# Wide edge one-hot compares on VectorE alone, and an fp32 gather of node rows, in a two-layer graph network kernel

## What is computed

```python
def layer0(x, src, dst, weight, bias):          # x is layernorm + relu of the input
    adj = zeros(256, 256); adj[src, dst] = 1; adj[dst, src] = 1; adj += eye
    dinv = 1 / sqrt(adj.sum(1))
    return (dinv[:, None] * adj * dinv[None, :]) @ (x @ weight) + bias

def layer1(x, idx_i=src, idx_j=dst, f=edge_attr_20, rcut=edge_weight, Yr=edge_attr_4):
    hs, hv = x[:, :128] @ w_in2f_s, einsum(x[:, 128:], w_in2f_v)     # 32 + 3*32 node channels
    s, v = hs[idx_j], hv[idx_j]                                     # gather: one row per edge
    W = (ssp(f @ W1 + b1) @ W2 + b2) * rcut                         # edge filters, 6 kinds x 32
    edge = [s*ys*W0, (v.yv)*W1, s*yv*W2, v*ys*W3, ...]
    agg = segment_sum(edge, idx_i, 256)                             # scatter: sum over edges
    return two dense layers of agg

x = x + layer0(relu(layernorm(x)), ...)
x = x + layer1(relu(layernorm(x)), ...)
```

## Time and profile before

| what | value |
|---|---|
| median of 3 runs (lowest, highest) | 89.17 us (88.24, 89.19) |
| profiled execution: span from its first to its last instruction | 86.5 us |
| median less that span | 2.7 us |
| busy: DVE, PE, POOL, PE weight loads, ACT | 73.4, 70.9, 55.1, 54.2, 40.6 us |
| share of the chain that ended last: DVE, PE, POOL, DMA | 57%, 17%, 5%, 6% |

### The profile page before, as it was taken

How to read it: one execution, slowest core, us unless ns; L and a number is a source line. 1 busy time by engine, 2 the same in 40 slices (tenths; PEclk the granted TensorE clock), 3 DMA queues, 4 the chain that set the end, 5 groups by cost and what they waited for, 6 DMA issues and landing times.

```text
span 86.5 us, 1513 instructions
## 1 busy us (share of the span) xinstructions
PE 70.9 (82%) x545; PEld 54.2 (63%) x545; DVE 73.4 (85%) x180; ACT 40.6 (47%) x60; POOL 55.1 (64%) x58
## 2 busy tenths in 40 slices
PE   4928999999359979999189999998778697999930
PEld 1204367388123536899089999996667595989620
DVE  1039999999997769998999999999999999992490
ACT  0140216929997025593702535271643639970520
POOL 2019999998940299989992789183664748970000
PEclk9999999999999999999965999999999999999996
DMA  2899999800000000000000000000000000000024
GB/s 8 249 319 368 373 438 426 312 0 0 0 0 8 0 0 0 0 0 0 0 0 8 0 0 0 0 8 0 0 8 0 0 0 0 8 4 0 0 91 152
DMA packets 3340, 6.01 MB, mean 69 GB/s; under 512 B 444, under 2 KB 2224, under 8 KB 3204
## 3 DMA queue, kind: packets, MB, share of 16 engines
q1 hardware_dynamic: 2274, 4.93, 16.2%
q10 hardware_dynamic: 1058, 0.98, 3.7%
HBM read 5.39 MB, written 0.52 MB: 68 GB/s over the span
## 4 chain that ended last, share of the span: by engine, by line
DVE 57%; PE 17%; issue 9%; DMA 6%; POOL 5%; ACT 2%; DVEq 0%; POOLq 0%
DVE onehot_dst L372 11%; DVE WY L174 8%; PE bank L682 7%; DMA idx_sb<-idx 6%; DVE WY L172 5%; DVE Os L371 4%; DVE WY L173 3%; DVE dst_bc L501 3%; DVE dst_bc L497 3%; PE bank L622 3%; POOL scales L335 2%; DVE dst_bc L494 2%; DVE dst_bc L495 2%; PE bank L640 2%; DVE Hp L466 2%
## 5 line engine op out<-in xcount | busy, mean ns | idle before, releaser
L682 PE MATMUL bank<-OsR,Mh 128*128 128x256 f32 x68 | 17.7, 297 | 3.3 <-POOL Ml L360 1.6
L682 PE MATMUL bank<-OsR,Ml 128*128 128x256 f32 x68 | 16.7, 281 | 0.0
L360 POOL TENSOR_TENSOR Ml<-dst_bc,Mh 128x512 fp32r<-128x512 f32 x8 | 10.3, 1283 | 9.4 <-ACT Mh L284 9.4
L682 PEld LDWEIGHTS bank<-OsR,Mh 128*128 128x128 f32 x68 | 12.8, 188 | 4.8 <-POOL Ml L364 2.4
L666 PE MATMUL bank<-Hp,onehot_dst 128*128 128x128 bf16 x204 | 14.0, 229 | 2.1 <-issue 2.1
L666 PEld LDWEIGHTS bank<-Hp,onehot_dst 128*128 128x128 bf16 x204 | 12.4, 103 | 2.7 <-issue 2.3
L548 PE MATMUL bank<-onehot_dst,Os 128*128 128x256 bf16 x68 | 10.0, 294 | 4.4 <-DVE onehot_dst L372 4.4
L372 DVE TENSOR_SCALAR onehot_dst<-iota_r,idf 128x256 bf16<-128x256 bf16 x27 | 13.0, 483 | 0.0
L682 PEld LDWEIGHTS bank<-OsR,Ml 128*128 128x128 f32 x68 | 12.8, 189 | 0.0
L548 PEld LDWEIGHTS bank<-onehot_dst,Os 128*128 128x128 bf16 x68 | 6.1, 102 | 8.9 <-DVE onehot_dst L372 7.7
L364 POOL TENSOR_TENSOR Ml<-dst_bc,Mh 128x512 fp32r<-128x512 f32 x7 | 10.4, 1492 | 1.3 <-ACT Mh L286 1.3
(11 more groups left out here) (116 smaller groups left out, 148.4 us busy)
## 6 DMA issues: line engine op xcount, KB each, us to landing
dst_bc<-dst_row SPq DMA_DIRECT2D x1, 2176.0 KB, 12.7
w_sb<-w SPq DMA_DIRECT2D x1, 1024.0 KB, 8.9
x_sb<-x SPq DMA_DIRECT2D x1, 512.0 KB, 5.6
...
idx_sb<-idx SPq DMA_DIRECT2D x1, 162.0 KB, 4.9
...
```

Of the source, the lines that this page charges most:

```text
L360: nc.gpsimd.tensor_tensor(Ml[:, o, 1, 0:n, :], M[:, o, 1, 0:n, :], Mh[:, o, 1, 0:n, :].bitcast(fp32), ALU.subtract).then_inc(q["MlB"], 1)
L682: last = nc.tensor.matmul(bank[4 + b][:, 0:N], part[:, g % RG, b, j, :], OsR[:, g % RG, j, :], start=(t == 0 and part is Mh), stop=(t == T ...
```

## The change

- All edge one-hots are made on DVE, by `tensor_tensor` instead of `tensor_scalar`: one instruction per matrix and wave, over 2, 4, 6, 8, 8, 4 and 2 tiles (`WAVES`). The numbers of the edges are bf16 in pairs (`idp`), so that both inputs end in a dimension of two neighbours. The node row comes ready from memory. One semaphore step per wave.
- The indices are first on SP's queue and smaller; the node row and `w1` go first on ACT's queue; `w1` no longer stands before `x`.
- GpSimd has no one-hots and no `hY`; it makes one extra power on a scratch tile at the start. DVE makes `hY`, after `hW_lo`.
- `OdT` is fp32, compared straight from the int32 row, with no bf16 copy. Its four calls stand after `hY`, and three in a row after `h2T`. The loop's first group has none behind it.
- `H` is scaled by ACT from PSUM to fp32 in SBUF, when `s2` is there; the gather is 2 fp32 matmuls per tile.
- ACT copies filter group 0 after the squares of `h2` instead of before; PE computes it after layer 0's product instead of before.
- `WY` is a ring of 6 groups.

```diff
     RW = 4
+    RY = 6
...
-    PT = T - 7
+    WAVES = ((0, 2), (2, 6), (6, 12), (12, 20), (20, 28), (28, 32), (32, T))
...
-        idx_sb = sb("idx_sb", [P, 2 * T + N], i32)
+        idx_sb = sb("idx_sb", [P, 2 * T], i32)
...
-        idf = sb("idf", [P, 2 * T])
+        idp = sb("idp", [P, 2 * T, 2], bf16)
...
-        dst_b = sb("dst_b", [P, E], bf16)
-        onehot_dst = sb("onehot_dst", [P, T * N], bf16)
-        Od = onehot_dst[:, :].rearrange("p (t n) -> p t n", t=T)
-        OdT = onehot_dst[:, :].rearrange("p (a e) -> p a e", a=NH)
+        OdT = sb("OdT", [P, NH, E])
+        Od = OdT[:, 0, :].bitcast(bf16).rearrange("p (t n) -> p t n", t=T)
...
-        Hr = sb("Hr", [P, NH, C])
-        Hp = [sb(f"Hp{i}", [P, NH, C], bf16) for i in range(3)]
+        H = sb("H", [P, NH, C])
...
-        WY = sb("WY", [P, T, S * F])
+        WY = sb("WY", [P, RY, TG, S * F])
...
         @block.sync
             sp.dma_start(idx_sb[:], idx).then_inc(d_idx, 16)
-            sp.dma_start(w1_sb[:], w1).then_inc(d_w1, 16)
             sp.dma_start(x_sb[:, :, :], x.rearrange("(a p) d -> p a d", p=P)).then_inc(d_x, 16)
...
         @block.scalar
+            act.dma_start(iota_r[:], iota).then_inc(d_iota, 16)
+            act.dma_start(w1_sb[:], w1).then_inc(d_w1, 16)
             act.dma_start(f_sb[:], f_t).then_inc(d_f, 16)
...
-            act.wait_ge(d_dst, 16)
-            nc.scalar.activation(dst_b[:], dst_bc[:], ACT.Copy).then_inc(q["dstb"], 1)
...
                 nc.scalar.activation(hW_hi[:, a, :], bank[a][:, :], ACT.Copy, scale=s1[:, a:a + 1]).then_inc(q["hW_hi"], 1)
-            filters_out(0)
             act.wait_ge(q["x1"], 1)
...
-            for g in range(1, 5):
+            for g in range(4):
                 filters_out(g)
+            act.wait_ge(q["s2"], 1)
+            for a in range(NH):
+                act.wait_ge(q["H"], a + 1)
+                nc.scalar.activation(H[:, a, :], bank[6 + a][:, 0:C], ACT.Copy, scale=s2[:, a:a + 1]).then_inc(q["Hs"], 1)
+            filters_out(4)
             scatter_onehots(2)
...
         @block.gpsimd
-            pool.wait_ge(q["idf"], 2)
-            for t in range(PT, T):
-                nc.gpsimd.tensor_scalar(Os[:, t, :], iota_r[:], idf[:, t:t + 1], None, ALU.is_equal).then_inc(q["onehot_p"], 1)
-                nc.gpsimd.tensor_scalar(Od[:, t, :], iota_r[:], idf[:, T + t:T + t + 1], None,
-                                        ALU.is_equal).then_inc(q["onehot_p"], 1)
+            nc.gpsimd.memset(scratch[:], 4.0).then_inc(q["half"], 1)
+            pool.wait_ge(q["half"], 3)
+            nc.gpsimd.tensor_tensor(scratch[:], scratch[:], neghalf[:], ALU.pow).then_inc(q["half"], 1)
...
-            pool.wait_ge(q["hhi"], 2)
-            nc.gpsimd.tensor_tensor(hY[0:64, :], za[64:128, :], hY[64:128, :].bitcast(fp32),
-                                    ALU.subtract).then_inc(q["hYlo"], 1)
...
         @block.vector
-            def onehots(t0, t1):
-                for t in range(t0, t1):
-                    nc.vector.tensor_scalar(Os[:, t, :], iota_r[:], idf[:, t:t + 1], None, ALU.is_equal).then_inc(q["onehot"], 1)
-                    nc.vector.tensor_scalar(Od[:, t, :], iota_r[:], idf[:, T + t:T + t + 1], None,
-                                            ALU.is_equal).then_inc(q["onehot"], 1)
+            def onehots(w):
+                t0, t1 = WAVES[w]
+                n = t1 - t0
+                nodes = iota_r[:].rearrange("p (h k) -> p h k", k=2).unsqueeze(1).broadcast_to((P, n, P, 2))
+                for first, into in ((0, Os), (T, Od)):
+                    of_edge = idp[:, first + t0:first + t1, :].unsqueeze(2).broadcast_to((P, n, P, 2))
+                    last = nc.vector.tensor_tensor(into[:, t0:t1, :].rearrange("p t (h k) -> p t h k", k=2), nodes, of_edge,
+                                                   ALU.is_equal)
+                last.then_inc(q["onehot"], 1)
...
-            nc.vector.tensor_copy(iota_r[:], idx_sb[:, 2 * T:]).then_inc(q["idf"], 1)
-            nc.vector.tensor_copy(idf[:], idx_sb[:, 0:2 * T]).then_inc(q["idf"], 1)
-            onehots(0, 6)
+            nc.vector.tensor_copy(idp[:, :, :], idx_sb[:, :].unsqueeze(2).broadcast_to((P, 2 * T, 2))).then_inc(q["idp"], 1)
+            dve.wait_ge(d_iota, 16)
+            dve.wait_ge(q["idp"], 1)
+            onehots(0)
+            onehots(1)
...
-            onehots(6, 16)
+            onehots(2)
+            onehots(3)
...
-            onehots(16, PT)
+            onehots(4)
+            onehots(5)
+            onehots(6)
...
-                nc.vector.tensor_scalar(OdT[:, a, lo:hi], dst_b[:, lo:hi], iota_c[:, a:a + 1], None,
+                nc.vector.tensor_scalar(OdT[:, a, lo:hi], dst_bc[:, lo:hi], iota_c[:, a:a + 1], None,
...
-            dve.wait_ge(q["hhi"], 1)
+            dve.wait_ge(q["hhi"], 2)
             nc.vector.tensor_tensor(hX[64:128, :], za[0:64, :], hX[0:64, :].bitcast(fp32), ALU.subtract).then_inc(q["hXlo"], 1)
-            dve.wait_ge(q["dstb"], 1)
-            node_onehots(0, 0)
             for a in range(NH):
                 dve.wait_ge(q["hW_hi"], a + 1)
                 nc.vector.scalar_tensor_tensor(hW_lo[:, a, :], bank[a][:, :], s1[:, a:a + 1],
                                                hW_hi[:, a, :].bitcast(fp32), ALU.mult, ALU.subtract).then_inc(q["hW_lo"], 1)
-            node_onehots(1, 0)
+            nc.vector.tensor_tensor(hY[0:64, :], za[64:128, :], hY[64:128, :].bitcast(fp32), ALU.subtract).then_inc(q["hYlo"], 1)
+            dve.wait_ge(d_dst, 16)
+            node_onehots(0, 0)
...
+            node_onehots(1, 0)
             node_onehots(0, 1)
-            dve.wait_ge(q["s2"], 1)
...
-            high(0)
-            rest(0)
...
+            node_onehots(1, 1)
             weight_filters(nc.vector, dve.wait_ge, 2)
...
+                if g == 0:
+                    dve.wait_ge(q["OdT"], 2 * NH)
                 dve.wait_ge(q["G"], g + 1)
...
-                if g == 0:
-                    node_onehots(1, 1)
-                elif g <= 4:
+                if 1 <= g <= 4:
                     weight_filters(nc.vector, dve.wait_ge, g + 4)
...
         @block.tensor
-            adjacency(range(0, 3))
+            adjacency(range(0, 2))
...
             hidden(0)
+            adjacency(range(2, 6))
             hidden(1)
...
                 if a == 0:
-                    adjacency(range(3, 5))
+                    adjacency(range(6, 9))
...
+            adjacency(range(9, 12))
             first_layer(0, 0, KD)
-            adjacency([5, *range(PT, T - 3), *range(6, 16), T - 3, T - 2, *range(16, 22), T - 1,
-                       *range(22, PT)])
+            adjacency(range(12, T))
             first_layer(1, 0, 1)
...
             first_layer(1, 1, KD)
-            filters(0)
...
+            filters(0)
             filters(1)
...
-                        for i in range(3):
-                            last = nc.tensor.matmul(gbank[g % RG][:, j * C:(j + 1) * C], OdT[:, a, t * P:(t + 1) * P],
-                                                    Hp[i][:, a, :], start=(a == 0 and i == 0), stop=(a == NH - 1 and i == 2))
+                        last = nc.tensor.matmul(gbank[g % RG][:, j * C:(j + 1) * C], OdT[:, a, t * P:(t + 1) * P], H[:, a, :],
+                                                start=(a == 0), stop=(a == NH - 1))
...
+        "iota": np.broadcast_to(np.arange(N).astype(bf), (P, N)),
```

More of the change, by code:

```diff
@@ L6, in gnn_preln_kernel @@
 def gnn_preln_kernel(nc, x, idx, dst_row, f_t, yr, w0, bias0, w1, w2, b2, w_in, w_o1s, w_o1vt, w_o2s, w_o2v,
-                     eye, ident_iota, out):
+                     eye, iota, ident_iota, out):
     fp32 = mybir.dt.float32
@@ L151, in gnn_preln_kernel, with wave @@
         q = {n: sem("s_" + n) for n in names.split()}
+        def wave(t):
+            return next(i for i, (t0, t1) in enumerate(WAVES) if t0 <= t < t1) + 1
         zb = (bank[2], bank[3], bank[7])
@@ L231, in _ @@
             nc.scalar.activation(hY[64:128, :], za[64:128, :], ACT.Copy).then_inc(q["hhi"], 1)
[L232 to L233 removed]
             def scatter_onehots(g):
                 t0, n = TG * g, tiles(g)
[L238 to L240 removed]
+                act.wait_ge(q["onehot"], wave(t0 + n - 1))
                 if g >= RG:
```

58 lines of the change are left out of this document (15 added, 43 removed).

## The result

The changed kernel takes 93.4 us (median of 4 runs, 92.66 to 94.67) where the kernel before takes 88.7: a ratio of 1.052 [1.042, 1.062]. The profiled execution took 92.86 us with a span of 90.8, so +4.3 of span against the 86.5 of before. The forecast was 90.8 us.

What follows compares the result with a forecast made beforehand. DVE bounds the kernel up to 26.7 us, then a relay of engines, then DVE again; after the change GpSimd's backlog decides group 2. 86.5 + 1.5 + 0.1 = 88.1 us span, with 2.7 around it 90.8 us; range 87.0 to 92.8.

Steps and rivals of the forecast that it cites:

- t0: End of the first power on GpSimd: 31.8 us before, forecast 27.6 after gains of 3.4 and 0.8.
- Part 1: Everything up to `CI`: wide compares, earlier transfers and no waiting beside GpSimd bring `CI` to 23.8 instead of 27.23, -3.4 us.
- Part 2: First power on GpSimd, read as held up by DVE's node compare, which no longer stands there: 0.8 us gained, bounds 0 and 1.25.
- That ends at 16.8 instead of 17.91: End of the early PE and ACT relay through the logarithm, after compare wave 2 and the second transposes.
- Part 3: From the first power to `x1`: `hY` and an fp32 node compare now stand between, `x1` at t0+5.0, +2.1 us.
- Part 4: Second power `s2`, behind group 0's filter products taking turns with node compares: at 43.1 instead of 39.05; first gather at 43.7.
- Part 5: GpSimd's backlog of products and splits after `s2` decides: group 2 on DVE at 56.1 instead of 54.59, +1.5 us.
- the clock costs nothing by itself: First gather on PE: even at full clock GpSimd's backlog sets group 2, so half clock adds 0 us.
- only then can DVE begin group 2: DVE starts group 2 only after GpSimd's four splits of groups 0 and 1, taken in turn with DVE's products, at 56.1.
- The draw: Rival: `s2` without intrinsic length, first power gaining 1.25 and `x` sooner each move t0 by 0.4 to 0.6; 89.3 us, chance 0.16.
- The one element a cycle: Rival: wide compares on DVE run at one element a cycle, `CI` at 29.0; 96 us, chance 0.07.
- The early gain: Rival: it passes through because node compares and GpSimd's products overlap, `s2` at 39.9; 87.7 us, chance 0.21.

Runs made afterwards that it cites:

- section 4: The kernel before with only the subtraction of the lower half of hX moved ahead of DVE's wait for the adjacency: 88.58 us, ratio 1.002.

## Why the prediction was wrong

The sign was right, and so was nearly all of the stretch behind t0; the time was 2.6 us too low because of Parts 1 and 2. They put t0 at 27.6 where it was 31.0. Two things made the miss look smaller, and both are luck: from t0 to group 2 it took 0.65 less than forecast, and the 2.7 around the span is 2.1 in every execution of the changed kernel.

**Part 1 (-3.4 forecast, -0.8 measured).** The rate was right: eight tiles and one matrix took 1.22 us (forecast 1.07 + 0.15), and from 1024 to 2048 elements it is 0.52 ns each. The Trainium skill, "VectorE: DVE Perf Modes", section on the perf-mode tier table, gives a bf16 `tensor_tensor` in SBUF two elements a cycle and 1224 ns for 2048 elements; the trace agrees with its 1.22 us. `x` was even earlier than I had it. The second half of the sum was right too: from the end of the logarithm to `CI` I had 7.0 us and it took 7.1. What failed is the step "That ends at 16.8 instead of 17.91": I ran the relay from wave 2 and the second transposes and never asked when `f` lands. The change put two transfers ahead of it, `hidden(0)` came at 9.34 instead of 8.22, and TensorE's clock was low under it and the matmuls behind it. The logarithm ended at 19.34, 2.5 us after the forecast, and that is nearly all of the 2.65 that `CI` missed. With TensorE kept busy 1.5 of it came back.

The other part of the -3.4 I had put down to the waiting beside GpSimd, and there the cause was right. Logarithm to `CI` is 9.3 us in the kernel before, 7.1 with the whole change and 7.0 to 7.2 with the narrow compares as soon as `hY` is off GpSimd. So the 2.55 of the earlier trace rows was the gain, and `hY`'s move alone takes it. The wide compares, on which the sum of Part 1 was built, are worth nothing on this stretch: in the kernel before the narrow ones are over at 17.0 and VectorE's small steps behind them at 17.9, when the logarithm ends, and after it the narrow ones with GpSimd's seven tiles are as fast.

**Part 2 (-0.8 forecast, 0 measured).** The step "I read them as held up by DVE's compare" failed. The power started 0.1 us after `hX` and ended 0.9 after `hX`'s end, in both kernels, and with `hX` out of its way it took 1.01. I had seen `hX` and let the nearer end decide. With the extra power on constants near the start (changed kernel) and without it (kernel before) that distance is the same 0.9, so the extra power bought nothing. (A compare that is running when the power starts does hold it: 1.46 in section 4.)

**Part 3 (+2.1 forecast).** Right: `x1` at t0+4.9 instead of t0+2.9; the node compare took 1.39, against 1.2.

**Part 4.** Right in kind and nearly in size: `s2` ended at t0+15.2 (forecast t0+15.5), with the products of group 0 held by the node compares. Inside it two errors cancel: the second power took 0.91 where I had 0.3, and VectorE's products, which I had put ahead of it with 0.8, did not delay it. By the Trainium skill, "SBUF — State Buffer", section "SBUF: two separate sides", the port pair of VectorE and GpSimd is locked for a whole instruction. For the products, the subtractions and the first power the trace agrees (0.62, 0.83, 0.83 became 1.65, 1.88, 1.87). For the second power it does not always: in the changed kernel it took 0.91 beside two of VectorE's products (45.09 to 46.09) that took 0.55 and 0.54, as short as elsewhere. The first gather came at t0+16.0 (t0+16.1) and took 3.65 (3.4).

**Part 5.** Group 2 at t0+27.85 (t0+28.5), GpSimd all but without a gap and group 2 behind the fourth split (58.05), as forecast. But "the clock costs nothing by itself" is refuted: at full clock group 2 came 1.6 us sooner, though GpSimd's backlog ended no sooner. There VectorE began group 2 at 57.64, before the fourth split was over (58.85). Its products of the next filters take turns with the splits, and with an earlier gather it reached them one split earlier. So "only then can DVE begin group 2" failed as a rule: how many splits it has to let pass depends on when the gather is done. The +0.1 behind group 2 was 0.0.

**Rivals.** The draw needed t0 to come sooner than forecast; it came 3.4 later. The one element a cycle was excluded by the 1.22. The early gain did not pass because only 0.8 of it existed and the products did take turns.
